# Scan and C product of one half after the other: VectorE's order inside a state of a selective-scan kernel

## What is computed

```python
def step(state, inp):
    ut, dtt, bt, ct = inp
    dA = jnp.exp(jnp.clip(dtt[:, :, None] * A, -5.0, 5.0))
    dB = dtt[:, :, None] * bt[:, None, :] * ut[:, :, None]
    state = dA * state + dB + 1e-06
    y = jnp.sum(state * ct[:, None, :], axis=-1) + D * ut
    return (state, y)
```

## Time and profile before

| | |
|---|---|
| median of 3 runs | 3001.63 us (2998.19 to 3005.22) |
| the profiled execution | 2997.44 us |
| its span, first to last instruction | 2995.7 us |
| busy: PE, DVE, ACT, POOL | 88%, 76%, 68%, 75% of the span |
| mean granted clock of TensorE | 0.917 of full speed |

### The profile page before, as it was taken

How to read it: one execution, slowest core, us unless ns; L and a number is a source line. 1 busy time by engine, 2 the same in 40 slices (tenths; PEclk the granted TensorE clock), 3 DMA queues, 4 the chain that set the end, 5 groups by cost and what they waited for, 6 DMA issues and landing times. The chain is left out here.

```text
span 2995.7 us, 55801 instructions
## 1 busy us (share of the span) xinstructions
PE 2625.7 (88%) x15616; PEld 2306.4 (77%) x15616; DVE 2262.1 (76%) x4890; ACT 2032.7 (68%) x4675; POOL 2237.3 (75%) x1354
## 2 busy tenths in 40 slices
PE   7888888888888888888888888888886599999998
PEld 4777777777777777777777777777875488888887
DVE  2999899889998998999889989999899233333332
ACT  3978888878877777878887888888876023333332
POOL 2989898989898888888898989898887033333333
PEclk9898998899998988999999999999897699999999
DMA  4222222222222222222222222222221278888886
GB/s 172 78 75 75 76 82 76 75 76 86 94 77 76 79 75 84 85 75 83 79 79 75 75 77 82 75 76 83 94 72 43 75 195 200 199 201 200 199 201 154
DMA packets 138194, 309.69 MB, mean 103 GB/s; under 512 B 15040, under 2 KB 79680, under 8 KB 137792
## 3 DMA queue, kind: packets, MB, share of 16 engines
q1 hardware_dynamic: 110848, 270.03, 28.7%
q0 software_dynamic: 27072, 36.46, 6.1%
HBM read 258.42 MB, written 48.01 MB: 102 GB/s over the span
## 5 line engine op out<-in xcount | busy, mean ns | idle before, releaser
L1035 POOL TENSOR_TENSOR room<-dtu,b_all 128x1024 f32<-128x1024 f32 x512 | 1202.1, 2371 | 33.8 <-DVE dtu L1421 14.0
L814 ACT ACTIVATE bank<-room,eps_col 128x512 f32<-128x512 f32 x1024 | 693.7, 683 | 336.8 <-DVE carry L1258 229.9
L801 ACT ACTIVATE room<-room,neg_a 128x256 f32<-128x256 f32 x2048 | 868.4, 498 | 7.5 <-DVE room L1244 5.1
L607 PE MATMUL bank<-ident,room 128*128 128x128 f32 x4096 | 552.0, 291 | 246.9 <-DVE room L1253 219.9
L607 PEld LDWEIGHTS bank<-ident,room 128*128 128x128 f32 x4096 | 496.2, 151 | 300.8 <-DVE room L1253 238.3
L1024 POOL TENSOR_TENSOR room<-room,c_all 128x1024 f32<-128x1024 f32 x224 | 532.0, 2375 | 167.9 <-ACT carry L819 105.6
L1244 DVE TENSOR_TENSOR_SCAN bank<-room,carry,bank 128x256 f32<-128x256 f32 x864 | 580.8, 736 | 56.8 <-ACT bank L814 47.8
L1160 POOL DMA_INDIRECT out<-room,ids x144 | 223.8, 1554 | 406.5 <-ACT room L995 235.9
L1323 DVE SCALAR_TENSOR_TENSOR hid<-hid,bank 128x256 f32<-128x256 f32 (+1 forms) x312 | 131.0, 420 | 446.9 <-ACT hid L908 446.9
L1244 DVE TENSOR_TENSOR_SCAN room<-room,carry,bank 128x256 f32<-128x256 f32 x672 | 448.1, 726 | 12.0 <-ACT bank L814 10.7
L559 PE MATMUL bank<-xnT,w_conv 128*128 128x256 f32 x3072 | 404.2, 288 | 7.0 <-ACT xnT L837 5.5
(11 more groups left out here) (150 smaller groups left out, 3141.0 us busy)
## 6 DMA issues: line engine op xcount, KB each, us to landing
b_all<-b_scratch SPq DMA_DIRECT2D x128, 512.0 KB, 3.9
c_all<-b_scratch SPq DMA_DIRECT2D x128, 512.0 KB, 5.4
room<-in_wgu SPq DMA_DIRECT2D x72, 704.0 KB, 5.6
room<-in_wd SPq DMA_DIRECT2D x72, 384.0 KB, 3.5
room<-x_by_expert SPq DMA_DIRECT2D x72, 260.0 KB, 2.9
x_in<-in_x SPq DMA_DIRECT2D x32, 256.0 KB, 5.5
x<-in_x SPq DMA_DIRECT2D x32, 256.0 KB, 2.7
out<-x SPq DMA_DIRECT2D x32, 256.0 KB, 4.1
```

The costliest lines, as they stand in the source:

```text
L607: last = mm(tr_bank[k][:, b * P:(b + 1) * P], v[n % VRING][:, b, k * P:(k + 1) * P], ident[:, :], is_transpose=True, start=False, stop=(n ...
L801: last = af(da[n % RING][:, b, :], dt[c.par][:, b, :], ACT.Exp, scale=neg_a[:, b, n:n + 1])
L814: af(v_slot(n, h)[:, :], v[n % VRING][:, 2 * h:2 * h + 2, :].rearrange("p b t -> p (b t)"), ACT.Identity, bias=eps_col[:, 0:1]).then_inc(v ...
L1035: nc.gpsimd.tensor_tensor(out=v[n % VRING][:, :, :], in0=dtu[:, :, :], in1=row, op=ALU.mult) \
```

## The change

The C product of a state used to follow the scans of both halves. Now each half's product and copy follow that half's two scans. `c_times_state` takes the halves that it is to do, and `scans` calls it after each half. The same instructions remain, and on the other engines nothing moves.

```diff
                         last = vec_e.tensor_tensor_scan(s, da[n % RING][:, b, :], p, init, ALU.mult, ALU.add)
                     last.then_inc(half_ready, 1)
+                    if n not in BY_POOL:
+                        c_times_state(c, n, (h,))
 
-            def c_times_state(c, n):
+            def c_times_state(c, n, part):
 
                 dve.wait_ge(c_loaded[n // NEAR], c.index * 16 + 16)
                 row = c_all[n // NEAR][:, n % NEAR:n % NEAR + 1, :].to_broadcast([P, 2, TC])
-                for h in range(2):
+                for h in part:
                     dve.wait_ge(half_ready, halves(c, n) + h + 1)
...
                         if scan:
                             scans(scan, slot, self.flag)
-                        if scan and slot not in BY_POOL:
-                            c_times_state(scan, slot)
```

## The result

| | before | after |
|---|---|---|
| median of 5 runs each, us | 3001.63 (2994.48 to 3005.22) | 3015.75 (3011.07 to 3019.89) |
| the profiled execution, its span, us | 2997.44, 2995.7 | 3013.64, 3011.9 |
| mean granted clock of TensorE | 0.917 | 0.908 |

The changed kernel takes 1.0051 times as long, with a 95% interval of 1.0038 to 1.0065: 14 us or 0.5% slower, where 3014 us was forecast.

What follows compares the result with a forecast made beforehand. VectorE was taken to bound states 12 to 15, TensorE states 7 to 11. Waits of 1.38 us less 0.95 of stalls gave +0.43 us per chunk, +13 us over 31 chunks: 3014 us, range 2992 to 3031.

Steps and rivals of the forecast that it cites:

- The price of a wait: VectorE, each product right behind its scans: an exposed wait of 0.23 us, 0.46 us per state with two products.
- the lost overlap: VectorE's back-to-back instructions overlap by 0.08 us; a product that waits loses this, in addition to its idle gap.
- The rival of a free wait: Ready semaphores cost nothing, so only the tanh stalls go: -0.95 us per chunk, 2972 us; chance 0.03.
- The tanh's stalls: VectorE's two waits for ScalarE's tanh, 0.40 and 0.39 us, vanish; with overlap this gives back 0.95 us per chunk.
- States 12 to 15: VectorE bounds this stretch: three states cost 1.38 us, the tanh stalls give back 0.95, net +0.43 us per chunk.
- Product 15 to the projections: Stretch into the next chunk: TensorE's chain stays, VectorE's slack absorbs its delay, 0 us; 0.24 us left over enter state 7.
- states 7 to 11: TensorE and its clip of delta hold the time: 0 us; 0.1 us allowed where the cover is gone.
- Product and stall exchanged at 7 and 9: The first product fills VectorE's stall for the second half's bank; states 7 and 9 each gain 0.43 us.
- The rival in which VectorE is the bound everywhere: TensorE's cover fails, all nine states count: +0.93 us per chunk, 3030 us; chance 0.20 together with a dearer wait.
- ScalarE's wait for the copies: Sign in the profile after: ScalarE's wait for VectorE's copies into carry falls from 230 us by over a third.

Runs made afterwards that it cites:

- `tanh_first`: The kernel before the change, with ScalarE's tanh of the shared expert moved ahead of its bank fill in slots 12 to 14: 2970.33 us against 2998.55, ratio 0.9902.
- `SPLIT = [15]`: The new order in state 15 alone, against the kernel before the change: 3012.97 us against 2997.56, ratio 1.0056.

## Why the prediction was right

**The price of a wait** was taken as 0.23 us between bounds of 0.12 and 0.29; it is 0.22 us, 0.44 us a state where 0.46 was reckoned. Two errors lie inside that nearly cancel: the idle time was to be 0.14 us and 80 us in all, and is 0.105 and 60.7 us, while the longer product and scan (0.025 us a product) were not in the sum. The reasoning (two semaphores, so a separate wait in front) pointed to the right side of the bounds, and the lost overlap was rightly counted. The rival of a free wait falls with the 40.9 us between two kernels that differ in the order alone. The Trainium skill, "VectorE: DVE Perf Modes", section "The DRAIN you can't avoid", says of eight copies with a semaphore after each that the semaphore costs nothing extra. For a product that waits for the scans right before it the trace does not agree: 60.7 us of idle time where 0.0 stood.

**The tanh's stalls** went, 0.95 us a chunk as forecast (1.01 us by `tanh_first`). Moving the tanh by itself gave 28 us, of which 30 periods at 0.81 us are 24.

**States 12 to 15** were to lose 0.43 us and lost 0.43. But 0.10 of that is the loop's turn, which the prediction did not have; its own terms came to 0.33 us. `SPLIT = [15]` showed that one state counts there in full.

**Product 15 to the projections, and states 7 to 11** were put at 0 each, with 0.24 us handed from the one to the other at state 7. There 0.22 us were handed over, and 0.30 came back: together -0.09 us, so the period of a chunk grew by 0.34 and not 0.43 us. Product and stall exchanged at 7 and 9 as described, and VectorE still waits at the clip and at the gate. It also waits for the logits now, a place that the prediction did not name. The cover in states 0 to 6 was what it took it to be. About states 7 to 11 it was too kind: with a wait in all nine states and no stall filled, +1.28 us came through. The rival in which VectorE is the bound everywhere was nearer than it looked.

**What the sum left out** was that the first chunk is not like the others: +3.6 us where it put 0.43. Nothing of another chunk's end stands beside it, and what VectorE is late there comes back larger through TensorE's clock. So 0.09 us a chunk too much, 2.8 us in all, and 3.2 us too little in the first chunk cancelled. That the total of +14 met the +13 so closely is luck.

**A sign that was missed:** ScalarE's wait for the copies was to fall by over a third from 230 us, and fell by 15%, to 195, in 166 waits instead of 152. A likely reason, not shown: the halves come free a microsecond sooner, but ScalarE, having less to wait for, arrives sooner too and waits again.

## What to carry to other kernels

An operation that reads what stands right before it on its own engine pays an idle gap and the overlap it had; count both, and for each occurrence look whether its stretch is bound by that engine, since one such state in the bound stretch cost as much as nine of them with a gain. When an edit gains only by making another engine's wait shorter, look for the instruction that is stuck behind that wait and move it instead: here the tanh ahead of the fill gave 28 us where the reordering lost 14. Treat cover as a stock that several small delays draw from. Count the first round of a loop by itself, and look at the loop's turn: an exposed wait ahead of the branch takes away the lead with which the branch was taken.

## What the runs showed of the hardware

**TensorE's slow periods move.** The two levels of its clock are 1.2 and 2.4 GHz, and the granted clock in windows of the scan phase lies between. In one chunk, with VectorE's order changed, the slow period stood elsewhere. Windows of before, then of after, at corresponding places (columns: stretch, length, busy us of PE, PEld, DVE, ACT, POOL with the instructions, granted clock, DMA share, GB/s):

```profile
1264.00:1272.00 8.00, 6.06 (x21) 5.26 (x21) 7.59 (x15) 6.68 (x15) 6.97 (x5) 0.55 0.55 167
1313.00:1320.00 7.00, 7.00 (x33) 5.71 (x34) 6.87 (x19) 6.68 (x19) 6.14 (x4) 0.76 0.61 176
```

```profile
1272.30:1280.30 8.00, 6.08 (x30) 5.63 (x31) 7.79 (x14) 7.99 (x18) 7.67 (x5) 0.70 0.57 168
1321.30:1328.30 7.00, 7.00 (x23) 6.02 (x23) 5.81 (x17) 5.30 (x14) 6.30 (x3) 0.51 0.76 236
```

TensorE's timelines there, before and after:

```profile
1267.70 4.47 PE L687 MATMUL bank<-w_dn,hid 128*128 128x256 f32 x12
...
1314.45 1.06 PE L651 MATMUL bank<-hot,ones 128*128 128x8 f32 x8
```

```profile
1275.98 3.31 PE L687 MATMUL bank<-w_dn,hid 128*128 128x256 f32 x12
...
1321.92 1.88 PE L651 MATMUL bank<-hot,ones 128*128 128x8 f32 x8
```

The down projection behind the wait for product 15 lies in a window with a granted clock of 0.70 instead of 0.55 and took 3.31 instead of 4.47 us; the small matmuls of the routing lie in one with 0.51 instead of 0.76 and took 1.88 instead of 1.06 us. On TensorE's timelines the stretch from the transposes of state 15 to the projection of B and C became shorter (28.75 to 27.76 us) and the one from there to the next such transposes longer (42.74 to 44.21 us), though no order of TensorE was touched. A stretch of one chunk read off two traces can therefore move by a microsecond to either side; the mean period over many chunks and the total are what may be compared. Over the whole scan phase the granted clock is 0.91 and 0.90. What of the +0.34 us a chunk would be there with an unmoved clock can't be told from these runs.

**The first chunk shows it in all twelve kernels.** Its eight matmuls of line 577 took 1.91 us in the six kernels in which TensorE had stood idle for 1.67 to 1.73 us before them, and 3.03 to 3.58 us in the six in which it had stood 2.13 to 2.59 us, all those with a wait more in states 1, 3 and 5. The idle time alone does not settle it: in the second chunk the same matmuls took 1.91 us in three kernels and 2.48 to 3.62 us in four others after idle times that were alike, 3.25 to 3.32 us.
